# Routed feed-forward on one core: keeping the lower expert's results beside their rows and scattering the sum with the higher expert's tiles

## What is computed

```python
x = x + attention(layernorm(x), ctx, ctx)
xt = layernorm(x)                                 # 8192 x 128
logits = xt @ gate_w.T
_, idx = top_k(logits + beta, 2)
c = zeros(8192, 8).at[rows, idx].add(sigmoid(logits at idx))
h = silu(xt @ gate_proj[e]) * (xt @ up_proj[e])   # 8 experts, hidden size 256
combined = sum over e of c[:, e] * (h @ down_proj[e])
x = x + combined + shared expert(xt)
```

## Time and profile before

| | |
|---|---|
| median of 3 runs | 427.84 us (426.01 to 429.95) |
| the profiled execution | 426.79 us, its span 425.1 us |
| mean granted TensorE clock | 0.956 |
| PE busy | 368.5 us, 87% of the span |
| POOL busy | 288.7 us, 68% |
| DVE busy | 258.6 us, 61% |
| ACT busy | 242.3 us, 57% |
| scatters of results (L569) | 103, 160.0 us |

### The profile page before, as it was taken

One profiled execution on the slowest core, in us unless ns is written; L12 is line 12 of the kernel. 1 busy time (PEld: TensorE's weight loads), 2 busy tenths in 40 slices (PEclk: granted clock), 3 DMA queues, 4 the chain that ended last, 5 costly groups with the idle time before them and its releaser, 6 DMA issues.

```text
span 425.1 us, 10724 instructions
## 1 busy us (share of the span) xinstructions
PE 368.5 (87%) x3165; PEld 304.6 (72%) x3165; DVE 258.6 (61%) x1114; ACT 242.3 (57%) x575; POOL 288.7 (68%) x319
## 2 busy tenths in 40 slices
PE   8887999999989968899970999999999999999600
PEld 3444766665566545589970999999999999999600
DVE  5777999897788577666540455556555556556300
ACT  3696979887778564156550455655656555655200
POOL 7758788786658757305540358888888388888883
PEclk9999999999989999999995899999999999999955
DMA  6964336873222112155653467777555255554432
GB/s 211 367 191 156 120 132 214 241 233 124 94 95 83 57 52 70 58 140 90 95 89 89 90 102 120 115 111 116 75 76 71 41 69 74 73 72 51 38 34 22
DMA packets 56296, 46.23 MB, mean 109 GB/s; under 512 B 6824, under 2 KB 45488, under 8 KB 56240
## 3 DMA queue, kind: packets, MB, share of 16 engines
q1 hardware_dynamic: 39360, 34.49, 29.1%
q0 software_dynamic: 16880, 11.05, 20.6%
HBM read 26.79 MB, written 22.48 MB: 116 GB/s over the span
## 4 chain that ended last, share of the span: by engine, by line
PE 53%; POOL 12%; issue 11%; SPq 8%; ACT 4%; another core or an unknown queue 3%; DVE 2%; DMA 2%; POOLq 1%; ACTq 0%; DVEq 0%
PE gu_pair L1673 24%; PE bank L1692 13%; SPq L386 4%; POOL out L569 4%; POOL sorted_rows L527 3%; POOL rstd L488 3%; PE bank L1592 3%; PE bank L1613 2%; PE bank L1650 2%; ACT rows L749 2%; PE bank L1601 2%; SPq L372 2%; PE gu_pair L1550 2%; SPq L355 1%
## 5 line engine op out<-in xcount | busy, mean ns | idle before, releaser
L569 POOL DMA_INDIRECT out<-t_out,tile_in x103 | 160.0, 1553 | 82.8 <-DVE t_out L1280 48.2
L1673 PE MATMUL gu_pair<-tile_T,W_slot 128*128 128x128 f32 x1120 | 137.8, 277 | 0.5 <-ACT tile_T L817 0.5
L1673 PEld LDWEIGHTS gu_pair<-tile_T,W_slot 128*128 128x128 f32 x1120 | 132.0, 194 | 0.7 <-issue 0.7
L1259 DVE SCALAR_TENSOR_TENSOR t_hid<-t_silu,gu_pair 128x512 f32<-128x512 f32 (+1 forms) x71 | 48.3, 680 | 80.1 <-ACT t_silu L838 42.7
L838 ACT ACTIVATE t_silu<-gu_pair 128x512 f32<-128x512 f32 (+1 forms) x71 | 41.9, 590 | 91.4 <-PE gu_pair L1673 84.9
L828 ACT ACTIVATE W_slot<-W 128x512 f32 x140 | 80.0, 621 | 8.9 <-issue 5.7
L527 POOL DMA_INDIRECT sorted_rows<-rows,slot x64 | 64.6, 1010 | 23.3 <-issue 21.0
L1692 PE MATMUL bank<-W_down,t_hid 128*128 x560 | 75.1, 277 | 0.0
L1692 PEld LDWEIGHTS bank<-W_down,t_hid 128*128 128x128 f32 x560 | 69.0, 194 | 0.2 <-issue 0.2
L1601 PE MATMUL bank<-xn_T,shared_gu 128*128 128x512 f32 x64 | 33.0, 609 | 1.5 <-ACT silu_g L813 1.4
L1613 PE MATMUL bank<-shared_dn,hid 128*128 128x128 f32 x256 | 33.0, 284 | 1.1 <-DVE hid L1115 1.1
(11 more groups left out here) (153 smaller groups left out, 466.6 us busy)
## 6 DMA issues: line engine op xcount, KB each, us to landing
tile_in<-sorted_rows SPq DMA_DIRECT2D x103, 65.5 KB
x_sb<-x SPq DMA_DIRECT2D x16, 256.0 KB, 4.2
c_T<-ctx_cols SPq DMA_DIRECT2D x16, 256.0 KB
c_sb<-ctx SPq DMA_DIRECT2D x16, 256.0 KB
out<-acc SPq DMA_DIRECT2D x16, 256.0 KB
sorted_rows<-sorted_rows SPq DMA_DIRECT2D x56, 65.5 KB
sorted_rows<-padding SPq DMA_DIRECT2D x1, 2096.0 KB, 14.0
out<-t_out,tile_in POOLq DMA_INDIRECT x103
```

The source lines that it names most:

```text
L569: e.indirect_dma_start(out_flat, bass.IndirectOffsetOnAxis(ap=tile_in[:, n % NR, ID:ID + 1].bitcast(I32), axis=0), t_out[:, n % NO], None, ...
L1259: e.scalar_tensor_tensor(out=t_hid[:, i % 2, 0:n * M], in0=t_silu[:, 0:n * M], scalar=0.5, in1=gate_up_pair[i % 2][1][:, 0:n * M], op0=ALU ...
L1673: r = e.matmul(bank[:, c:c + P], W_slot[:, i % TX, h, at:at + P], tile_T[:, i % TX, tile], start=True, stop=True, skip_group_check=True)
```

## The change

A token is in one lower and in one higher tile. Before, both results were added to `out` by an indirect DMA of their own. Now the result of a lower tile is stored to the second half of its rows' places in `sorted_rows` (`store_part`); the copies that make the higher lists take their rows from the lower lists, with those results beside them; a higher tile loads both halves, DVE adds the stored result to its own, and POOL scatters the sum. So:

- The table has two rows (`STRIDE` = 2) for each place: row and result. A lane has 2 x 8192 rows (`LANE`), where before places of different pairs lay between each other at a stride of 32 rows. The blank rows are written to the beginning of each lane.
- The order is 15 whole tiles, 17 lower items, 14 whole ones, 17 higher items, 8 whole ones.
- SP stores the result of lower tile n when it comes to the load of tile n + 15 (`BEHIND`). After the last store and its landing it fills the higher lists in one go, before the load of the first higher tile.
- Copies run in turns of four chains instead of one round over all lists, and `find_parts` decides which row numbers are loaded together. A copy for a higher list moves 256 rows of the table, as 16 pieces.
- The padding tiles lie in the buffers of x and are set to zero once the first phase is done.
- Lower tiles are not scattered. POOL drains only after tile 14.

```diff
-    STRIDE = 32
+    STRIDE = 2
     STEP = STRIDE * P
+    LANE = STRIDE * N
+    WIDE = STRIDE * ROW
     LISTS = E - 1
     SPAN = -(-(LISTS * (P - 1) + P) // P)
-    NONE = P + Q + 2 + STEP
+    NONE = P + (Q + 2) * LANE + STEP
     NONES = LISTS * (P - 1) // P
     PADS = LISTS + NONES
-    LAST = P + STRIDE * N - STEP
+    LAST = P + (Q + 3) * LANE - STEP
     def list_base(k, l):
-        return P + Q + k + STEP * (1 + SPAN * l)
-    assert Q + 3 <= STRIDE and 1 + SPAN * LISTS <= N // P and NONES + 1 < N // P
...
-    HEAD = 14
-    TAIL = 1
-    assert PADS < HEAD
-    order = [(0, p) for p in range(HEAD)]
-    for k in (1, 2):
-        among = (FULL - HEAD - TAIL) // 2
-        for d in range(DUALS):
-            order.append((k, d))
-            if (d + 1) * among // DUALS > d * among // DUALS:
-                order.append((0, sum(kind == 0 for kind, _ in order)))
-    for _ in range(TAIL):
-        order.append((0, sum(kind == 0 for kind, _ in order)))
-    assert sum(kind == 0 for kind, _ in order) == FULL
+    HEAD, MID = 15, 14
+    assert PADS < HEAD and HEAD + MID < FULL
+    lowers, highers = [(1, d) for d in range(DUALS)], [(2, d) for d in range(DUALS)]
+    wholes = [(0, p) for p in range(FULL)]
+    order = wholes[:HEAD] + lowers + wholes[HEAD:HEAD + MID] + highers + wholes[HEAD + MID:]
...
+        padding = x_sb[:, :, :, :].rearrange("p r t d -> p (r t d)")[:, 0:PADS * WIDE].rearrange("p (n w) -> p n w", n=PADS)
...
+        tile_in = sb("tile_in", [P, NR, WIDE])
...
+        def parts_in_turn(k):
+            longest = sorted(range(LISTS), key=lambda l: -parts_of(k, l))
+            turn = [[(r, l) for r in range(parts_of(k, l))] for l in longest]
+            ways = LISTS // 2 + 1
+            run = turn[:ways]
+            for later, first in zip(turn[ways:], reversed(run)):
+                first.extend(later)
+            return [run[w][r] for r in range(LISTS) for w in range(ways)]
+        parts = [parts_in_turn(k) for k in range(2)]
+        assert all(sorted(parts[k]) == sorted((r, l) for l in range(LISTS) for r in range(parts_of(k, l))) for k in range(2))
         def added(n):
-            return 16 * (n // NR + 1)
+            return 16 * sum(m not in partial for m in range(n % NR, n + 1, NR))
+        def wait_done(e, n):
+            if n in partial:
+                s = partial.index(n)
+                e.wait_ge(s_part_out[s % NS], 16 * (s // NS + 1))
+            else:
+                e.wait_ge(s_t_added[n % NR], added(n))
+        NI, NS = 12, 4
+        partial = [n for n in range(TILES) if order[slot_with[n]][0] == 1]
...
-        DRAINED = (HEAD - 1, 58)
+        BEHIND = 15
...
+            def rows_of(at, pieces=P):
+                return sorted_rows[bass.DynSlice(at, STEP), :].rearrange("(p c) w -> p (c w)", p=pieces)
             def load_tile(n):
                 if n == 0:
                     for g in range(G - RR, G):
                         e.wait_ge(s_scattered[g % RR], scatters(g))
                 if n >= NR:
-                    e.wait_ge(s_t_added[n % NR], added(n - NR))
-                if order[slot_with[n]][0] and tiles[slot_with[n]][0] == n and order[slot_with[n]][1] == 0:
-                    k = order[slot_with[n]][0] - 1
+                    wait_done(e, n - NR)
+                if n >= NI:
+                    e.wait_ge(s_t_in[n % NI], 16 * (n // NI))
+                kind, d = order[slot_with[n]]
+                if kind and d == 0 and tiles[slot_with[n]][0] == n:
                     for l in range(LISTS):
-                        e.wait_ge(s_listed[l], listed(k, l, parts_of(k, l) + 1))
+                        e.wait_ge(s_listed[l], listed(kind - 1, l, parts_of(kind - 1, l) + 1))
                     e.wait_ge(s_none_out, 16 * (1 + NONES))
-                e.dma_start(tile_in[:, n % NR], sorted_rows[bass.DynSlice(rows_at[n], P, STRIDE), :]).then_inc(s_t_in[n % NR], 16)
+                w = WIDE if kind == 2 else ROW
+                e.dma_start(tile_in[:, n % NR, 0:w], rows_of(rows_at[n])[:, 0:w]).then_inc(s_t_in[n % NI], 16)
+            def store_part(n):
+                s = partial.index(n)
+                e.wait_ge(s_t_out, n + 1)
+                if s >= NS:
+                    wait_done(e, partial[s - NS])
+                e.dma_start(rows_of(rows_at[n])[:, ROW:WIDE], t_out[:, n % NO]).then_inc(s_part_out[s % NS], 16)
...
+            def find_parts(k, r, l):
+                some = [m for m in (range(l, LISTS // 2 + 1) if l <= LISTS // 2 else range(l, LISTS)) if r < parts_of(k, m)]
+                e.wait_ge(s_part_row, 2)
+                to = row_numbers(part_row[0:1, k, r, l:l + len(some)])
+                part_at.update(zip([(k, r, m) for m in some], to))
             def copy_part(k, c):
                 r, l = parts[k][c]
                 if (k, r, l) not in part_at:
-                    some = [m for m in range(l, LISTS) if (r, m) in parts[k]][:4]
-                    e.wait_ge(s_part_row, 2)
-                    to = row_numbers(part_row[0:1, k, r, l:l + len(some)])
-                    part_at.update(zip([(k, r, m) for m in some], to))
+                    find_parts(k, r, l)
                 if k or r:
                     e.wait_ge(s_listed[l], listed(k, l, r))
-                e.dma_start(sorted_rows[bass.DynSlice(part_at[k, r, l], P, STRIDE), :],
-                            sorted_rows[bass.DynSlice(P + part_of(k, r, l), P, STRIDE), :]).then_inc(s_listed[l], 16)
+                if k == 0:
+                    e.dma_start(rows_of(part_at[k, r, l])[:, 0:ROW], rows_of(P + part_of(k, r, l) * LANE)[:, 0:ROW]
+                                ).then_inc(s_listed[l], 16)
+                else:
+                    e.dma_start(rows_of(part_at[k, r, l], 16), rows_of(part_at[0, l - r, r], 16)).then_inc(s_listed[l], 16)
...
-            copied, padded = [0, 0], [0, 0]
-            def fill_lists(k, m):
-                for _ in range(m):
-                    if copied[k] < len(parts[k]):
-                        copy_part(k, copied[k])
-                        copied[k] += 1
-                    elif padded[k] < LISTS:
-                        pad_list(k, padded[k])
-                        padded[k] += 1
+            def fill_lists(k):
+                for c in range(len(parts[k])):
+                    copy_part(k, c)
+                for l in sorted(range(LISTS), key=lambda l: max(c for c, part in enumerate(parts[k]) if part[1] == l)):
+                    pad_list(k, l)
+            stored = 0
             for n in range(TILES):
+                while stored < len(partial) and partial[stored] + BEHIND <= n:
+                    store_part(partial[stored])
+                    stored += 1
+                    if stored == len(partial):
+                        for m in partial[-NS:]:
+                            wait_done(e, m)
+                        fill_lists(1)
...
-                if n >= HEAD:
-                    fill_lists(1, 1)
...
-                if order[i] == (1, 0) and n == tiles[i][0]:
+                if order[i] == (2, 0) and n == tiles[i][0]:
                     for m in range(PADS):
-                        e.wait_ge(s_t_added[m], added(m))
-                if order[i] == (2, 0) and n == tiles[i][0]:
-                    last = max(m for m in range(n) if order[slot_with[m]][0] == 1)
-                    for m in range(last - NR + 1, last + 1):
-                        e.wait_ge(s_t_added[m % NR], added(m))
+                        wait_done(e, m)
...
-                e.memset(padding[:, FILL:PADS], 0.0).then_inc(s_const, 1)
-                e.wait_ge(s_const, 16)
...
+            e.wait_ge(s_x2, G)
+            e.memset(padding, 0.0).then_inc(s_padding, 1)
             e.drain()
             for n in range(TILES):
-                add_to_out(n)
-                if n in DRAINED:
+                if n not in partial:
+                    add_to_out(n)
+                if n == HEAD - 1:
...
+                        y_h, weight = y[:, h * D:(h + 1) * D], tile_in[:, n % NR, WT + kind - 1:WT + kind]
                         free_out(n)
-                        e.tensor_scalar(t_out[:, n % NO], y[:, h * D:(h + 1) * D], tile_in[:, n % NR, WT + kind - 1:WT + kind], None,
-                                        ALU.mult).then_inc(s_t_out, 1)
+                        if kind == 1:
+                            e.tensor_scalar(t_out[:, n % NO, 0:D], y_h, weight, None, ALU.mult).then_inc(s_t_out, 1)
+                        else:
+                            e.scalar_tensor_tensor(out=t_out[:, n % NO, 0:D], in0=y_h, scalar=weight, in1=tile_in[:, n % NR, ROW:ROW + D],
+                                                   op0=ALU.mult, op1=ALU.add).then_inc(s_t_out, 1)
```

More of the change, by code:

```diff
@@ L112, in build @@
         list_step = sb("list_step", [P, 2, LISTS])
-        padding = sb("padding", [P, PADS, ROW])
+        blank = sb("blank", [P, FILL, ROW])
         beta_all = sb("beta_all", [P, E])
@@ L294, in build @@
```

(29 more changed lines are left out.)

25 lines of the change are left out of this document (12 added, 13 removed).

## The result

The changed kernel took 443.71 us in the median of 4 runs (439.98 to 446.85) beside 427.06 us of the kernel before in the same series (426.01 to 429.95): ratio 1.0298 [1.0228, 1.0367], slower. The forecast was 430.0 in a range up to 436.

The account below looks back on a forecast made before the run. POOL's scatters set the end: first higher result at 346.1 us, plus 0.1, 75.8 for 41 scatters and 6.0 gives span 428.0, less 0.5 for small edits. That is 2.4 over before, added to the median: 430.0, range 418 to 436.

Parts of the forecast that it names:

- first filling: SP's 28 copies making the lower lists, before the first lower pair: 10 register loads, paddings starting at 216.8 us.
- the 0.5 of the small edits: At the kernel's beginning: the removed padding memset of 1.03 us gains 0.5 us, between 0 and 1.
- first rival: SP's copy issue in the second filling keeps 0.52 us, 3.9 us more, 434 us in all; chance 0.25.
- The first hole: TensorE's idle time before the first lower pair: 7 us, restart at 230.5 us, 2.6 us sooner.
- The last store: After the last lower result at 288.0 us: store 0.25, landing 1.77, and waits for four stores, to 290.1.
- The blank rows: Write at the beginning, 3584 pieces instead of 1024 for the same bytes; 3 us of delay would be hidden.
- Paddings of the second filling: Seven padding writes on SP after the copies, 5.3 us with two loads; last issued at 328.9, landed at 330.7.
- second filling: SP's 28 copies making the higher lists after the last lower result, each with its own load: 33.8 us, to 323.9.
- the cover of 14 tiles: Whole tiles keeping TensorE at work during the second filling, to 320.1 us, 32.1 after the last lower result; then 13.6 waiting.
- The rival that the chain of copies binds: In the second filling, long-row copies land after more than 4.8 us; at 5.5 us, 5 us more, 435; chance 0.10.

Follow-up runs that it names:

- again: The changed kernel run once more with no edit, on chip 1: 441.4 us, ratio 1.0321 to the kernel before.
- pieces128: Changed kernel with the 28 copies of the second filling as 128 pieces instead of 16, same bytes: 427.57 us, ratio 1.0314 to the kernel before.
- empties_early: Changed kernel with the six empty tiles written after copy 14 of the first filling, not behind the paddings: 427.17 us, ratio 1.0297 to the kernel before.
- loads_ordered: Changed kernel with the second filling's chains taking turns in opposite order, 17 register loads instead of 28: 437.43 us, ratio 1.0258 to the kernel before.
- best1: Changed kernel with loads_early, empties_early, 18 whole tiles first, 16 in the middle, stores 17 behind, fewer padding loads: 414.23 us, ratio 0.9972 to the kernel before.
- mid20: Changed kernel with 20 whole tiles instead of 14 between lower and higher items: 444.48 us, ratio 1.0408 to the kernel before.
- behind19: Changed kernel with stores 19 tiles behind instead of 15, 18 middle tiles instead of 14, store row numbers reloaded: 424.04 us, ratio 1.0213 to the kernel before.
- loads_early: Changed kernel with the order of loads_ordered and 12 second-filling row numbers loaded during lower tiles: 427.34 us, ratio 1.0314 to the kernel before.

## Why the prediction was wrong

The mechanism came out as forecast, and several of its sizes did not. On the way to the first higher result the forecast and "again" compare like this (us; the last column is what the step itself adds to the lateness):

| step of the forecast | forecast | measured | added |
|---|---|---|---|
| first filling, paddings, empty tiles, restart of TensorE | 230.5 | 234.03 | +3.5 |
| last lower result | 288.0 | 292.04 | +0.5 |
| store, landing, waits, to the first load of the filling | 290.1 | 295.46 | +1.3 |
| 28 loads and 28 copies | 323.9 | 331.88 | +2.6 |
| paddings with their loads, landing, two tile loads, restart | 333.7 | 343.00 | +1.3 |
| first higher result | 346.1 | 356.24 | +0.8 |
| POOL's last scatter ended | 422.0 | 432.36 | +0.2 |
| behind it, and the 0.5 of the small edits | 427.5 | 439.2 | +1.3 |

- **The step that failed**: "The DMA instruction now has 16 long rows on either side ... I take 0.38". It was 0.52, the upper bound, which the forecast had as its first rival at 0.25: 28 x 0.14 = 3.9 us more. The loads cost what was forecast (12.9 us for 12.8), and the gaps beside a copy and its load came to 0.32 in the mean, (36.4 - 12.9 - 14.6) / 28, instead of 0.37, which gives 1.3 back: 36.4 us instead of 33.8, the +2.6 of the table. I gave the number of rows a weight against the kind of the transfer. "pieces128" shows that their number makes no difference here (521 ns for 16 and for 128), and the row of before with the same kind of transfer already had 524. This alone gives the rival's 434.
- **The first hole**: the other large miss, and of the same size. The forecast took the landing of the last empty tile from before, 1.77. It was 4.16: 13 tiles of 134 KB are written within 9 us where they were 13 of half the size. That is 2.4 of the 3.5 us. The rest is the filling. Its copies ended at 217.14, with one DMA instruction of 1.10 instead of 0.52 (215.03) and small waits, and then the first padding's row numbers had to be loaded (217.19, 0.87), which the forecast's 216.8 leaves out; so the paddings began at 218.53. Of these 1.7 us 0.3 were given back before the last empty tile and 0.3 behind it. "empties_early" took the landing back to 2.38.
- **The last store**: in the lower stretch SP was "hidden", but the last result found it still busy, with a store that took 1.07 us instead of 0.36, a register load and a tile load. The last store went 1.33 us after the result; the forecast let SP stand ready.
- **The blank rows**: the forecast was that "3 us of delay would be hidden". They were issued at 10.6 and landed 19.4 us later against 14.0, and POOL waited 3.84 us. The bytes were not the same either, as the forecast had it, but fewer: 1834 KB against 2096. The first router scatter began at 30.24, before at 29.45. Nothing is left of the gain of 0.5 at the beginning: the first scatter of a result stands at 192.16 against 192.03.
- **Paddings of the second filling**: from the end of the copies to the issue of the last padding 5.5 us passed instead of 5.0 (one load of row numbers took 1.13), the last padding landed after 2.38 instead of 1.77, and the restart came 0.2 later behind that: the +1.3.
- **An error of sum**: 427.84 + 2.4 is 430.2 and not 430.0. It changes nothing.
- **Right**: 70 scatters with POOL busy over the last 41 of them (75.8 forecast, 75.84 measured); two holes with the second at the end of the cover; the cover of 14 tiles; 28 loads of their own in the second filling, with their prices (confirmed by "loads_ordered"); the landing of a copy hidden by its turn, until the loads went ("best1"); TensorE's clock at 0.50 at the end of the second hole; no cost of the memset, nor of the add on DVE (347 ns in the row of "mid20"). The rival that the chain of copies binds did not happen in this kernel.

Nearly all sizes erred to the same side. Most of the errors were stalls that the trace of before did not have, and each time I took the value of the calmer row. Together the errors outside the named rivals sum to about 8 us (11.7 of the span less the 3.9 of the copies), and the range had only a microsecond or so for them. The range had room for the 3.9 but not for the 8.

**What was given back and why the change loses.** Taking 33 scatters off POOL was real (61.3 us with their gaps). But it made the copies of the higher lists depend on the last lower result. In the kernel before, they went one by one between tile loads beside other work; now they are 36.4 us of SP's issue behind the last lower result. With the store before them and the paddings and tile loads behind them SP needs 51 us from that result to the restart (292.04 to 343.00), and the 14 tiles of cover give TensorE work for 32 of these. With that issue cut, covered and started earlier ("best1"), the changed kernel is 3.7% shorter (ratio 1.035 to 0.9972), which leaves 0.3% against the kernel before.

**Open.** Why the blank rows are slow; whether the late last store of "behind19", "loads_early" and "best1" is wholly the wait for landings or partly the added register loads (both are in all three); and how much of "best1" each of its parts gives. Moving second-filling copies between the lower pairs, which would shorten the part on the path, was not run: where a list's rows end is known only from the data, so a general order of copies that needs only the early results was not at hand.

## What to carry to other kernels

When work is taken off the engine that sets the end, write down what the new dependence holds back, and on which queue: here a list of 28 copies became unable to start before the last result. Price a DMA's issue from a row of the same kind of transfer, here between DRAM and DRAM, and not from one that shares only its number of rows, and a landing by what lands with it, not by a row where it was alone. Additional cover counts only as far as its own loads are ahead of the stall in the queue ("mid20").

## What the runs showed of the hardware

- SP's issue of a DMA between DRAM and DRAM with two register addresses takes 0.52 us with 16 rows of 8 KB as with 128 rows of 1 KB (521 ns both, "again" and "pieces128"). With one register address and a source that is known beforehand it is no less: 524 ns in the median of the first filling of "again". A tile load and a padding take 0.33.
- In "again" a write of 134 KB from SBUF to DRAM landed 4.16 us after its issue when it was the last of 13 within 9 us, and after 2.38 when it was the last of 7 (337.36); "empties_early" has 2.38 for the last of 7 too, "best1" 3.66 (317.75). From 226 to 230 us in "again" the DMA engines were busy for 0.93 of the time, at 234 GB/s.
- One write of 1.9 MB in 3584 pieces of 524 bytes, one for each row of 28 lanes that lie 8.6 MB apart, beside the loads of the first phase: 19.4 us to land. In "again" the share of the 16 DMA engines (next to last column) reads above 1 in that time, at 121 to 201 GB/s (last column); the kernel before had 1.06 at 383 GB/s from 16 to 20 us and 1.06 at 284 from 20 to 24:

```profile
16.00:20.00 4.00, 3.90 (x46) 2.07 (x44) 3.62 (x27) 2.20 (x8) 2.60 (x6) 1.00 1.24 201
20.00:24.00 4.00, 2.96 (x20) 1.40 (x20) 2.83 (x18) 4.00 (x16) 2.51 (x4) 1.00 1.39 121
24.00:28.00 4.00, 3.91 (x52) 2.59 (x50) 3.02 (x23) 3.76 (x11) 1.14 (x2) 1.00 1.20 174
```

- Of the three chips two ran the kernel before in 415 us and one in 427.7.
